# First cross-attention of a two-layer gated model: latents normalised and transposed with the context, batch by batch

## The reference

```python
x = x + tanh(g_xattn[0]) * L0_xattn(ctx, layernorm(x), ...)      # first cross-attention
x = x + tanh(g_ffn[0])   * L0_ffn(layernorm(x), ...)             # experts, 2 of 8 a row
x = x + tanh(g_xattn[1]) * L1_xattn(layernorm(x), ctx, ctx, ...)
x = x + tanh(g_ffn[1])   * L1_ffn(layernorm(x), ...)

def L0_xattn(x, latents, gamma_x, beta_x, gamma_l, beta_l, Wq, Wkv, Wo):   # x is the context here
    xn = layer_norm(x, gamma_x, beta_x)
    ln = layer_norm(latents, gamma_l, beta_l)      # so the latents are normalised twice
    q = (ln @ Wq) / 8                              # 8 heads of 64
    k_x, v_x = split(xn @ Wkv); k_l, v_l = split(ln @ Wkv)
    k = concat(rope(k_x), k_l); v = concat(v_x, v_l)   # 375 + 112 = 487 columns
    return (softmax(q k^T) v) @ Wo
```

## Time and profile before

| | |
|---|---|
| median of 3 runs | 862.2 us (861.44 to 862.49) |
| profiled execution | 856.11 us, its span 854.3 us |
| TensorE busy | 789.1 us, 92% of the span |
| VectorE, ScalarE, GpSimd busy | 464.3 (54%), 350.2 (41%), 164.8 (19%) |
| chain that ended last | 76% TensorE, 11% VectorE, 6% DMA |
| mean granted TensorE clock | 0.986 of full speed |

### The profile page before, as it was taken

How to read it: one execution, slowest core, us unless ns; L and a number is a source line. 1 busy time by engine, 2 the same in 40 slices (tenths; PEclk the granted TensorE clock), 3 DMA queues, 4 the chain that set the end, 5 groups by cost and what they waited for, 6 DMA issues and landing times.

```text
span 854.3 us, 14115 instructions
## 1 busy us (share of the span) xinstructions
PE 789.1 (92%) x5024; PEld 541.0 (63%) x5024; DVE 464.3 (54%) x1160; ACT 350.2 (41%) x934; POOL 164.8 (19%) x232
## 2 busy tenths in 40 slices
PE   0499999999999999999999997999999988999998
PEld 0345665555565665888998875756666655555567
DVE  2466667666665330122222229577888886776642
ACT  0355555456556411332223323486666652111110
POOL 4311322132000061000000027213343310100000
PEclk9999999999999999999999998999999998999999
DMA  7422252211111783366455332500000000000001
GB/s 212 163 65 54 54 159 61 54 46 35 41 28 24 254 298 95 118 226 210 157 183 181 130 94 65 198 1 2 2 1 2 2 2 1 0 1 1 1 11 33
DMA packets 43418, 69.71 MB, mean 82 GB/s; under 512 B 6500, under 2 KB 34925, under 8 KB 43093
## 3 DMA queue, kind: packets, MB, share of 16 engines
q1 hardware_dynamic: 41812, 65.14, 24.2%
q0 software_dynamic: 1536, 3.67, 1.4%
HBM read 52.56 MB, written 8.26 MB: 71 GB/s over the span
## 4 chain that ended last, share of the span: by engine, by line
PE 76%; DVE 11%; DMA 6%; issue 3%; POOL 2%; SPq 1%; ACT 1%; DVEq 0%; POOLq 0%
PE ps L1265 11%; PE ps L1711 9%; PE ps L1504 7%; PE ps L1516 6%; PE ps L1316 6%; PE ps L1319 6%; PE ps L1597 5%; PE ps L1356 4%; DMA OT<-slot_rows 3%; PE ps L1435 3%; PE ps L1748 3%; PE ps L1376 3%; PE ps L1424 3%; PE ps L1622 2%; PE ps L1306 2%
## 5 line engine op out<-in xcount | busy, mean ns | idle before, releaser
L1265 PE MATMUL ps<-ident,arena 112*125 112x112 f32 (+5 forms) x776 | 108.2, 277 | 28.1 <-POOL arena L396 18.9
L1265 PEld LDWEIGHTS ps<-ident,arena 112*125 112x125 f32 (+5 forms) x776 | 87.2, 164 | 60.0 <-issue 35.2
L679 ACT ACTIVATE OT<-ps,bt 128x128 f32<-128x128 f32 x168 | 48.0, 369 | 113.7 <-PE ps L1504 112.8
L1711 PE MATMUL ps<-arena 128*112 128x384 f32 x256 | 91.2, 497 | 0.3 <-DVE acc L1092 0.3
L708 ACT ACTIVATE arena<-ps,negmax 112x375 f32<-112x375 f32 x128 | 73.3, 572 | 42.9 <-DVE negmax L853 42.0
L1504 PE MATMUL ps<-OT,arena 128*128 128x128 f32 x672 | 80.2, 279 | 0.4 <-DVE OT L990 0.4
L1504 PEld LDWEIGHTS ps<-OT,arena 128*128 128x128 f32 x672 | 78.4, 195 | 0.7 <-issue 0.6
L1516 PE MATMUL ps<-arena,OT 128*128 128x256 f32 x336 | 75.8, 379 | 0.0
L853 DVE TENSOR_REDUCE negmax<-ps 112x1 f32<-112x375 f32 x128 | 63.8, 541 | 20.6 <-PE ps L1597 19.0
L848 DVE TENSOR_REDUCE negmax<-ps 112x1 f32<-112x487 f32 x64 | 39.5, 660 | 58.6 <-PE ps L1356 58.5
L1004 DVE COPY yo<-ps 128x256 f32<-128x256 f32 x21 | 8.9, 425 | 108.9 <-PE ps L1516 108.9
(11 more groups left out here) (237 smaller groups left out, 1245.8 us busy)
## 6 DMA issues: line engine op xcount, KB each, us to landing
arena<-in_up_w SPq DMA_DIRECT2D x21, 1024.0 KB, 5.2
arena<-in_down_w SPq DMA_DIRECT2D x8, 1024.0 KB, 12.2
arena<-arena SPq DMA_DIRECT2D x128, 60.9 KB, 2.0
arena<-in_wqkv SPq DMA_DIRECT2D x1, 3072.0 KB, 12.8
arena<-in_ctx SPq DMA_DIRECT2D x8, 375.0 KB
slot_rows<-acc SPq DMA_DIRECT2D x3, 896.0 KB, 8.6
OT<-slot_rows SPq DMA_DIRECT2D x21, 128.0 KB, 4.9
slot_out<-yo SPq DMA_DIRECT2D x21, 128.0 KB, 1.7
```

What stands on the lines that cost most here:

```text
L679: act.activation(he[:, i % 2, m, :], ps[:, 2 * (i % 2) + m // 4, (m % 4) * SLOT:(m % 4 + 1) * SLOT], ACT.Gelu, bias=bt[:, i % 3, m:m + 1]) ...
L1265: return pe.transpose(dst, src, ident[0:k, 0:k])
L1711: ins = pe.matmul(ps[0:TQ, g % 4, 0:384], xb[p][:, c, :], wqkv[:, c, 2 * g:2 * g + 2, :].rearrange("p e n -> p (e n)"), start=(c == 0), st ...
```

## The change

SP loads batch 0 of `x` by itself, first; the other seven come after wkv, wq, cos and sin. The semaphores of these loads are split, so that each user waits for its own. The statistics, the deviations and the two normalisations of the latents are done one batch at a time: batch 0 ahead of the loop, batch n+1 on VectorE in step 0 of batch n. The latents' two transposes go into the PSUM banks of the context's (`l0_t1`), and ScalarE copies them to `kvin` from there; so `xn_T`, `xnT_out`, `latents` and their semaphores go, and `l0_q` waits for both copies of `l0_t1`. The context is normalised by ScalarE (`ctx_hat`) from two values that GpSimd forms (`ctx_rstd`), at the end of step 3 for the context two batches on. In the prelude the first k product comes ahead of q. The statistics of context 1 move from the prelude to step 0 of batch 0, and its normalisation to step 1. ScalarE runs a small exp at its very start.

```diff
@@ SP
-            sp.dma_start(x[:, :, :], a["x"].rearrange("b q d -> q b d")).then_inc(s_x, 16)
+            sp.dma_start(x[:, 0, :], a["x"][0, :, :]).then_inc(s_x0, 16)
...
-            sp.dma_start(wq, a["wq"].rearrange("(c p) n -> p c n", p=P)).then_inc(s_w0, 16)
-            sp.dma_start(cos_t[:, :], a["cos"]).then_inc(s_const, 16)
-            sp.dma_start(sin_t[:, :], a["sin"]).then_inc(s_const, 16)
             sp.dma_start(wkv, a["wkv"].rearrange("(c p) n -> p c n", p=P)).then_inc(s_w0, 16)
+            sp.dma_start(wq, a["wq"].rearrange("(c p) n -> p c n", p=P)).then_inc(s_wq, 16)
+            sp.dma_start(cos_t[:, :], a["cos"]).then_inc(s_trig, 16)
+            sp.dma_start(sin_t[:, :], a["sin"]).then_inc(s_trig, 16)
+            sp.dma_start(x[:, 1:, :], a["x"][1:, :, :].rearrange("b q d -> q b d")).then_inc(s_x, 16)
...
@@ GpSimd
-            ctx_norm(0, 0)
-            tile_rstd(0)
-            tile_rstd(1)
-            pool.wait_ge(s_xte, B)
-            latents(0, 0)
-            ctx_norm(1, 1)
-            latents(1, 1)
+            def latents_rstd(n, k):
+                pool.wait_ge(s_lstat, 2 * n + k + 1)
+                link(pool.tensor_scalar(veps[:, n:n + 1], mv[:, n, 1:2], EPS, None, ALU.add))
+                pool.tensor_tensor(rstd[:, n:n + 1], veps[:, n:n + 1], mhalf[0:TQ, 0:1], ALU.pow).then_inc(s_lrstd, 1)
+
+            def ctx_rstd(n):
                 pool.wait_ge(s_cstat, n + 1)
...
+                link(pool.tensor_scalar(vepsc[:, :], mvc[:, :, 1], EPS, None, ALU.add))
+                link(pool.tensor_tensor(rstdc[:, :], vepsc[:, :], mhalf[0:CR, 0:3], ALU.pow))
+                link(pool.tensor_tensor(nmrc[:, :], mvc[:, :, 0], rstdc[:, :], ALU.mult))
+                pool.tensor_scalar(nmrc[:, :], nmrc[:, :], -1.0, None, ALU.mult).then_inc(s_crstd, 1)
...
@@ ScalarE
+            def ctx_hat(n, p):
+                act.wait_ge(s_crstd, n + 1)
+                if n >= 2:
+                    act.wait_ge(L0["t1"], (n - 1) * KC)
+                for t in range(3):
+                    ins = act.activation(hat[p][:, t, :], cx[p][:, t, :], ACT.Identity, scale=rstdc[:, t:t + 1],
+                                         bias=nmrc[:, t:t + 1])
+                ins.then_inc(s_hat, 1)
...
-                    act.activation(kvin[p][:, c, 0:TK], ps[:, l0_bank("t1", n, c), 0:TK], ACT.Identity,
-                                   scale=affine[:, 0, c:c + 1], bias=affine[:, 1, c:c + 1]).then_inc(L0["t1e"], 1)
+                    bank = l0_bank("t1", n, c)
+                    act.activation(kvin[p][:, c, 0:TK], ps[:, bank, 0:TK], ACT.Identity,
+                                   scale=affine[:, 0, c:c + 1], bias=affine[:, 1, c:c + 1])
+                    act.activation(kvin[p][:, c, TK:NK0], ps[:, bank, TK:NK0], ACT.Identity,
+                                   scale=affine[:, 2, c:c + 1], bias=affine[:, 3, c:c + 1]).then_inc(L0["t1e"], 1)
...
+                if n == 0 and u == 1:
+                    ctx_hat(1, 1)
+                if n + 2 < B and u == 3:
+                    ctx_hat(n + 2, p)
...
@@ VectorE, in l0_step
                 softmax_max(L0, g + 1, 2 * u + 1, NK0)
+                if n + 1 < B and u == 0:
+                    if n == 0:
+                        dve.wait_ge(s_x, 16)
+                    latents_stats(n + 1, x, 0)
                 if u < 3:
                     l0_rope(n, u + 1)
                 elif n + 1 < B:
                     l0_rope(n + 1, 0)
+                if n + 1 < B and u == 0:
+                    latents_stats(n + 1, xn, 1)
                 softmax_norm(L0, g, 2 * u, probs, NKP0)
...
                 softmax_norm(L0, g + 1, 2 * u + 1, probs, NKP0)
+                if n + 1 < B and u == 0:
+                    latents_norm(n + 1)
+                if n == 0 and u == 0:
+                    ctx_stats(1, 1)
...
@@ TensorE
             def l0_t1(n, p):
                 pe.wait_ge(s_hat, n + 1)
+                pe.wait_ge(s_ln, n + 1)
...
-                        ins = T(ps[:, bank, t * CR:(t + 1) * CR], hat[p][:, t, c * P:(c + 1) * P], CR)
-                    ins.then_inc(L0["t1"], 1)
+                        T(ps[:, bank, t * CR:(t + 1) * CR], hat[p][:, t, c * P:(c + 1) * P], CR)
+                    T(ps[:, bank, TK:NK0], xn[:, n, c * P:(c + 1) * P], TQ).then_inc(L0["t1"], 1)
...
             def l0_q(n, p):
-                pe.wait_ge(s_lat, n + 1)
+                pe.wait_ge(L0["t1e"], (n + 1) * KC)
...
             l0_t1(0, 0)
-
-            pe.wait_ge(L0["t1e"], KC)
-            xn_T(0, 0)
-            pe.wait_ge(s_xte, B)
-            pe.wait_ge(s_w0, 16 * N_W0)
+            pe.wait_ge(s_w0, 16)
+            l0_kv(0, 0, 0, ("k",))
+            pe.wait_ge(s_wq, 16)
             l0_q(0, 0)
-            l0_kv(0, 0, 0)
+            l0_kv(0, 0, 0, ("v",))
             l0_kv(0, 0, 1)
```

More of the change, by code:

```diff
@@ L524, in _ @@
         def _(act):
[L525 to L539, removed]
+            act.wait_ge(s_fill, N_FILL)
+            act.activation(am[:, 3:4], ones[0:TQ, 0:1], ACT.Exp)
+            def ctx_hat(n, p):
[6 more added lines that the diff above has]
+                ins.then_inc(s_hat, 1)
             def l0_t1(n, p):
@@ L631, in l0_step @@
                     l0_r(n - 2)
+                if n == 0 and u == 1:
+                    ctx_hat(1, 1)
+                if n + 2 < B and u == 3:
+                    ctx_hat(n + 2, p)
+            act.wait_ge(s_cx[0], 16)
+            ctx_hat(0, 0)
+            act.wait_ge(s_const, 32)
             l0_t1(0, 0)
-            xnT_out(0, 2, 3)
+            l0_k(0, 0)
             l0_q(0, 0)
-            for j in (0, 1):
-                l0_k(0, j)
-                l0_v(0, 0, j)
+            l0_v(0, 0, 0)
+            l0_k(0, 1)
+            l0_v(0, 0, 1)
             for n in range(B):
@@ L813, in residual, with latents_stats @@
-            def residual(k, g, bias):
-                dve.wait_ge(s_tanh, 1)
-                for t in range(B):
-                    dve.wait_ge(s_op, k * B + t + 1)
-                    src = ps[0:TQ, t, 0:D]
-                    if bias is not None:
-                        link(dve.tensor_tensor(xn[:, t, :], src, bias[0:TQ, :], ALU.add))
-                        src = xn[:, t, :]
-                    ins = dve.scalar_tensor_tensor(x[:, t, :], src, tgate[0:TQ, g:g + 1], x[:, t, :], ALU.mult, ALU.add)
-                link(ins)
+            def latents_stats(n, src, k):
+                if k:
+                    dve.wait_ge(s_lrstd, 2 * n + 1)
+                    link(dve.tensor_scalar(xn[:, n, :], x[:, n, :], mv[:, n, 0:1], rstd[:, n:n + 1], ALU.subtract, ALU.mult))
+                link(dve.bn_stats(st6[:, n, :], src[:, n, :]))
+                dve.bn_aggr(mv[:, n, :], st6[:, n, :]).then_inc(s_lstat, 1)
@@ L825, in _, with latents_norm @@
+            def latents_norm(n):
+                dve.wait_ge(s_lrstd, 2 * n + 2)
+                dve.tensor_scalar(xn[:, n, :], xn[:, n, :], mv[:, n, 0:1], rstd[:, n:n + 1], ALU.subtract, ALU.mult)\
+                   .then_inc(s_ln, 1)
             dve.wait_ge(s_fill, N_FILL)
+            dve.wait_ge(s_x0, 16)
+            latents_stats(0, x, 0)
             ctx_stats(0, 0)
-            dve.wait_ge(s_x, 16)
-            tile_stats(x)
-            tile_norm(0, x, last=False)
-            tile_stats(xn)
@@ L1308, in l0_q, with l0_kv @@
                 ins.then_inc(L0["q"], 1)
-            def l0_kv(n, p, j):
+            def l0_kv(n, p, j, kinds=("k", "v")):
                 pe.wait_ge(L0["t1e"], (n + 1) * KC)
-                for kind in ("k", "v"):
+                for kind in kinds:
                     bank = l0_bank_free(kind, n, j)
@@ L1787, in begin, with prelude @@
         return ("t1", n, 0), ("t1", n, 1), ("q", n, 0)
+    def prelude():
+        return ("t1", 0, 0), ("t1", 0, 1), ("k", 0, 0), ("q", 0, 0), ("v", 0, 0)
     def pair(n, j):
         return ("k", n, j), ("v", n, j)
-    seq.extend(begin(0) + pair(0, 0) + pair(0, 1))
+    seq.extend(prelude() + pair(0, 1))
     for n in range(B):
```

114 lines of the change are left out of this document (39 added, 75 removed).

## The result

The changed kernel takes 888.16 us (median; 883.54 to 889.67, 4 runs), the kernel before 862.35 beside it (861.44 to 863.83, 4 runs): ratio 1.0289, 95% interval 1.0254 to 1.0323. The profiled execution took 883.54 us, with a span of 881.8 against 854.3, so the traces differ by 27.5 us. The mean granted clock is 0.967 (0.986 before). Both profiled executions are shorter than their medians, so trace is compared with trace and median with median.

A forecast was written before the change was run, and what follows sets the result against it. TensorE, busy 92% of the span, bounds the kernel. Span 854.3 - 9.4 (prelude) + 15.9 (q's waits) + 0 (VectorE) + 6.5 (batch 0) + 8.5 (clock) = 875.8; 21.5 more, on the median 883.7 us; range 869 to 893.

The forecast's parts named there:

- a: Rival: q's wait stays but the clock does not fall in batches 1 to 7; 876.9 us; chance 0.26.
- b: Rival: the clock stays low for longer, or GpSimd answers late in step 0; 895 us; chance 0.12.
- c: Rival: swap not held up, SP there by 20, first scores at 26, gain 21.7; 858.8 us; chance 0.08.
- d: Rival: first context comes no earlier, landing near 11.9; same time as the forecast, counted within its 0.50.
- The prelude's gain: Before the first scores: they start at 38.3 instead of 47.70, a gain of 9.4 us (7.5 to 13.0).
- TensorE's own chain: Prelude: k, q, v, k, v through near 26; by TensorE alone the first scores would gain 21.7 us.
- SP reaches the swap near 29.2, landed 36.8: Prelude: SP issues k's half-swap DMAs only behind all its loads; landing bounds 33.2 to 38.7.
- s(0,0): Start of the scores of batch 0, step 0, in s(batch, step) notation; forecast 38.3 instead of 47.70.
- The wait of q: Step 2: q waits for ScalarE's copies, 2.65 us for each of batches 2 to 7, 15.9 in all.
- The clock: TensorE's clock falls to half after idle ahead of q: one in batch 0, four later, 1.7 each; 8.5 us.
- VectorE's step 0: Added statistics and norms in step 0 of steady batches: cost 0, up to 0.4 a batch if GpSimd is late.
- Batch 0: First batch, counted from its first scores: step 3 scores at 26.1 instead of 19.6; 6.5 us (4.5 to 8).

The follow-up runs named there:

- e3: Changed kernel with 14 of SP's 18 small loads and its six bulk loads put behind the first half-swaps of k; 874.22 us, ratio 1.0142.
- after: The changed kernel itself, as measured beside the kernel before; 888.16 us, ratio 1.0289.
- e7: Changed kernel with all of x loaded first in one DMA again, ahead of context 0; 887.44 us, ratio 1.0292.
- e1: Changed kernel with ten unread products on TensorE ahead of q's wait, in batches 1 to 7; 878.47 us, ratio 1.0191.
- e2: Changed kernel with the next batch's transposes and ScalarE's copies moved from step 2 to the end of step 1, batches 2 to 7; 864.21 us, ratio 1.003.
- e8: Changed kernel with ScalarE copying the latents' columns of both chunks first and q waiting for these alone; 872.94 us, ratio 1.0112.
- e4: Kernel before with one added wait: q also waits for ScalarE's two copies of the transposed context, batches 1 to 7; 885.42 us, ratio 1.0265.
- e5: Changed kernel with the edits of e2 and e3 together; 851.17 us, ratio 0.9859.
- e6: e5 with batch 1's context and latents statistics and norms in the prelude, and its transposes at the end of step 1; 847.84 us, ratio 0.986.
- e9: e6 with VectorE's order changed: statistics of context 1 and first of latents 1 between the first rope's cos and sin multiplies; 843.84 us, ratio 0.9771.

## Why the prediction was right, and where it was off

The forecast was 883.7 us, +21.5 on trace and median alike; the trace shows +27.5, and the medians differ by 25.8. The mechanism stood: a gain in the prelude that the swap cuts short, and a wait ahead of q in each batch that costs twice, by itself and by the clock. No rival decided it: the clock did fall (against a), it did so about as often as forecast (against b in the steady batches), the swap was held up (against c), and the context did come early, used at 6.85 against 7.5 (against d). Step by step:

**The prelude's gain was mis-sized: 5.9, not 9.4.** This is most of the miss. TensorE's own chain was right (through at 25.8, forecast 26; 26.09 in e3). The context's way to the first transposes was right too. The failing step is "SP reaches the swap near 29.2, landed 36.8". SP reached it at 31.83. I had added 0.45 for the one more load and taken the other issues as they were, but how long single issues took shifted: in the kernel before the long ones were 4.38 (`gate`), 1.67 (context 1) and 2.81 us (`w1k`), in after 2.10, 3.38 and 2.60, with 3.86 for the small `gbias` and 1.50 for `w1o` in place of some half a microsecond. The sum came out 3.0 us longer. e7, with x in one load, reaches the swap at 28.80, and the four with x in two loads and the same list at 30.34 to 31.83 (after, e1, e2, e8); so the added 1.5 to 3.0 go with the split load, and what lengthens a single issue, no run shows. And the swap was used 5.7 us after its last issue had ended (34.59 to 40.29), three times the 1.9 that I took from the slot-clearing stores. The engines were still full, as the stretches of after show (the number ahead of the last is the DMA share):

```profile
32.00:36.00 4.00, 0.00 (x0) 0.00 (x0) 0.00 (x0) 0.00 (x0) 0.00 (x0) 0.50 1.09 357
36.00:41.00 5.00, 0.00 (x0) 0.00 (x0) 0.67 (x2) 0.00 (x0) 0.00 (x0) 0.50 0.88 234
```

I had let them run out before 36, as in the kernel before, though SP was late with the last loads. Part of the later stretch is the load of context 2, which SP issues at 34.64, right behind the swap; which of the bytes hold the swap is not shown. The gain of 5.9 lies outside the bounds that I gave (7.5 to 13.0), because the lower one left out that the two delays come together. It was not one odd execution: in the four other kernels with the late swap (e1, e2, e7, e8) it was used 5.5 to 6.2 us after its last issue, and s(0,0) was 39.55 to 41.45.

**The wait of q was right.** TensorE idle 2.27 (forecast 2.44), the two added transposes 0.36 (0.2); together 2.63 against 2.65, and 2.45 to 2.72 by the batch lengths. The copies took 0.54, 0.33 and 0.55 from start to start and 0.48 for the last: 1.90 against 1.91. The Trainium skill (ScalarE: Activation LUTs, section "What ACT_TABLE_LOAD costs") gives a fixed time for an instruction and one for each column, and an addition for each operand that is read per partition, as scale and bias are here; from these I work out an estimate of 0.69 and 0.47 us for 375 and 112 columns; the trace's durations of 0.67 to 0.69 and 0.46 to 0.48 us agree.

**The clock was right in number, too low in price.** Forecast: one fall in batch 0 and four in the other six, at 1.7. Seen: just that. The exact count is partly luck, as nothing in the forecast says in which batches it falls: the same wait gave falls in five of the six later batches in e3 and in four of six in e7. Three cost 1.65, the last 3.3 (over 6 us at half clock, as at 700 in the earlier trace rows). Six batches: 24.4 against 22.7. e1 shows that idleness is the cause, since ten products in the idle time took the falls of batches 1 to 6 away and left the wait. Over the kernels with such waits ahead of q the falls go with the idle: none in 4 at 1.16 to 1.17 us (e8), 17 in 25 between 1.85 and 2.35 (after, e3, e4, e7, e8), the one at 2.79 (e1), all 8 from 3.06 up (after, e2, e3, e5, e7, e8). The rule that I weighed, of the Trainium skill (TensorE: Matmul & The Clock Gate, section "Why this matters for your kernels"), would have idle gaps of all but the longest of these lengths harmless; the measurement decides against it here. Which of two batches with the same 2.27 us loses the clock, no run here explains.

**VectorE's step 0: nothing, as forecast.** In steady batches the steps 0, 1 and 3 are as long as before.

**Batch 0: 8.9 against 6.5 and 1.7 for its fall.** s(0,1) came 6.7 behind s(0,0) (6.3 forecast), s(0,2) 12.9 (13.35), q 21.7 (20.8), s(0,3) 28.6 (26.1). TensorE was idle 5.00 ahead of q where I had 3.7; s(0,2) was counted 0.4 too late, and together the batch missed the sum by 0.7. e6 and e9 take this wait away: batch 0 comes to 27.97 and 25.02.

**What the change is worth by its parts.** By the medians, the early transposes take 24 off the changed kernel (e2), the early swap 14 by itself (e3) and 13 when added to e2 (e5; 15 by the ratios). Both together turn 1.0289 into 0.9859. Of the change as it stood, the earlier first load brought nothing (e7). The traces say less than the medians in two cases: s(7,3), the end of the stage, is at 294.74 in after, 273.78 in e2 (21.0 earlier), 286.86 in e3 (7.9), 258.87 in e5 (35.9). The rest of the span, which no experiment touches, took 587.0 us in the kernel before and 587.1 to 597.2 in the ten others, so a whole time of one execution says little about a few microseconds in the stage.

## What to carry to other kernels

A wait that is put in front of the bound engine costs its length each time round, and it can cost as much again in clock (1.65 to 3.3 us behind an idle of 2.27 here): look at what stands between the two sides of the wait, and issue the producer one step earlier (e2). Before crediting a faster data path, follow the queue that issues its next DMA, SP here, in program order, and move what nobody needs yet behind what is waited for (e3); one more load in that queue can cost more than its own issue of 0.7 us (1.5 to 3.0 us here). And place new work of an in-order engine in a gap that it has anyway, not ahead of the step others wait for (e6, e9).

## What the runs showed of the hardware, unexpected

- A swap of four SBUF-to-SBUF DMAs, 60.9 KB each, was used 1.5 us after its last issue in e3 (issues 19.75 to 22.27, use at 23.75). Behind 3 MB of bulk loads it took 5.5 to 6.2 us (after, e1, e2, e7, e8).
- An issue on SP, 0.43 us as a rule, took up to 3.86 us for a small load in after and up to 4.38 in the kernel before. While the one of 3.86 lasted (15.81 to 19.67) the DMA share fell from 1.13 to 0.32, so full DMA engines alone do not explain it.
- The clock does not follow from the length of the idle alone: with the same 1.85 or 2.27 us it fell in some places and not in others, and in later stages it fell after 1.58 us in the kernel before and stayed after 1.55 in e6. Executions of one kernel scatter with such waits and without: by 12.7 us in e8 (867.45 to 880.16), and by 11.2 in the kernel before beside e5 to e8 (857.97 to 869.21, 7 runs).
